# Rows of the split operands start behind 2 edge elements instead of 16, and both samples' rows get the edge

## The reference

```
ctx   = causal_ema(x, tau_ctx)
wg    = sigmoid([x, ctx] @ Wg.T + bg)
gated = x * wg
mod   = 0.5 + sigmoid(gelu(x @ Wn1.T + bn1) @ Wn2.T + bn2)     # 8 rates
temporal = sum over d of blend_d * causal_ema(gated * mod_d, tau_d)
gate  = sigmoid(temporal @ Wtemp.T + btemp)
soma  = gelu(x @ Wsoma.T + bsoma)
x     = x + layernorm((soma * gate) @ Wout.T)                  # stage 1

s0, s1, s2 = relu(x @ share_wi[i]) @ share_wo[i]               # F = 1024
expert_out = two experts of four, picked by the sample's type, weighted
g     = softmax(relu([first tokens] @ gate_w1) @ gate_w2)
x     = x + g0 * expert_out + g1 * s0 + g2 * s1 + g3 * s2      # stage 2
```

## Time and profile before

| | |
|---|---|
| median of 3 runs | 1089.53 us (1088.98 to 1089.96) |
| profiled execution | 1089.96 us |
| its span, first to last instruction | 1087.5 us |
| instructions | 12453, of them 4754 matmuls |
| granted TensorE clock | 1.00 on the mean |

### The profile page before, as it was taken

The page is one execution under the profiler, slowest core; times in us unless marked ns, Lnnn a source line. Parts: engine busy times, 40 slices in busy tenths (PEclk is TensorE's granted clock), DMA queues, the critical chain, the costliest instruction groups (busy, mean ns, idle before and its releaser), DMA issues.

```text
span 1087.5 us, 12453 instructions
## 1 busy us (share of the span) xinstructions
PE 1067.4 (98%) x4754; PEld 861.6 (79%) x4754; DVE 764.0 (70%) x1245; ACT 399.1 (37%) x628; POOL 8.9 (1%) x20
## 2 busy tenths in 40 slices
PE   8799999999999999999999999999999999999998
PEld 6388777888888888888888888888888888888886
DVE  7979987499654995469863896549955598545234
ACT  6454455422334233332344223432234323322231
POOL 0000000000000000000000000000000000000000
PEclk9999999999999999999999999999999999999999
DMA  6359888676444564546544564545645465446550
GB/s 219 112 198 388 304 322 303 240 292 254 143 170 160 206 254 155 175 154 255 190 155 155 198 249 172 189 160 194 234 152 194 155 237 209 144 168 220 184 193 19
DMA packets 36476, 219.58 MB, mean 202 GB/s; under 512 B 4354, under 2 KB 4610, under 8 KB 14786
## 3 DMA queue, kind: packets, MB, share of 16 engines
q1 hardware_dynamic: 34114, 206.22, 52.5%
q0 software_dynamic: 2304, 12.58, 3.1%
HBM read 185.10 MB, written 33.69 MB: 201 GB/s over the span
## 4 chain that ended last, share of the span: by engine, by line
PE 81%; DVE 16%; issue 1%; ACT 1%; DMA 0%; DVEq 0%
PE ps_up L583 12%; PE ps_up L585 12%; PE ps_up L584 11%; PE ps_down L584 11%; PE ps_down L585 11%; PE ps_down L583 11%; PE ps_aux L583 3%; PE ps_aux L585 3%; PE ps_aux L584 3%; DVE trace L1162 3%; DVE hid_lo L1065 3%; DVE trace L1193 2%; DVE temporal L1202 1%; DVE wi L1057 1%; PE ps_down L727 1%
## 5 line engine op out<-in xcount | busy, mean ns | idle before, releaser
L1065 DVE SCALAR_TENSOR_TENSOR hid_lo<-ps_up,hid_hi 128x512 fp32r<-128x512 f32 x320 | 219.5, 689 | 268.0 <-ACT hid_hi L863 266.2
L863 ACT ACTIVATE hid_hi<-ps_up 128x512 fp32r<-128x512 f32 x320 | 192.0, 600 | 544.9 <-PE ps_up L585 544.5
L583 PE MATMUL ps_up<-x_hi_all,wi 128*128 128x512 f32 (+1 forms) x644 | 256.6, 398 | 0.1
L585 PE MATMUL ps_up<-x_hi_all,wi 128*128 128x512 f32 (+1 forms) x644 | 253.5, 394 | 0.0
L583 PE MATMUL ps_down<-hid_hi,wo 128*128 128x512 f32 x640 | 250.6, 392 | 1.7 <-DVE hid_lo L1065 1.1
L584 PE MATMUL ps_down<-hid_lo,wo 128*128 128x512 f32 x640 | 250.9, 392 | 0.0
L585 PE MATMUL ps_down<-hid_hi,wo 128*128 128x512 f32 x640 | 250.5, 391 | 0.0
L584 PE MATMUL ps_up<-x_lo_all,wi 128*128 128x512 f32 (+1 forms) x644 | 249.8, 388 | 0.0
L583 PEld LDWEIGHTS ps_down<-hid_hi,wo 128*128 128x128 f32 x640 | 120.2, 188 | 31.0 <-issue 3.2
L585 PEld LDWEIGHTS ps_up<-x_hi_all,wi 128*128 128x128 f32 x644 | 120.7, 187 | 30.1
L584 PEld LDWEIGHTS ps_down<-hid_lo,wo 128*128 128x128 f32 x640 | 120.5, 188 | 27.8
(11 more groups left out here) (202 smaller groups left out, 836.8 us busy)
## 6 DMA issues: line engine op xcount, KB each, us to landing
wi<-split_wi SPq DMA_DIRECT2D x70, 1024.0 KB, 4.8
wo<-split_wo SPq DMA_DIRECT2D x70, 1024.0 KB, 4.9
modb<-mod_scratch SPq DMA_DIRECT2D x28, 512.0 KB, 4.4
split_wi<-wi SPq DMA_DIRECT2D x10, 1024.0 KB, 6.6
split_wo<-wo SPq DMA_DIRECT2D x10, 1024.0 KB, 8.2
xt<-in_x SPq DMA_DIRECT2D x8, 512.0 KB, 6.0
split_wi<-ex POOLq DMA_DIRECT2D x4, 1024.0 KB, 7.9
split_wo<-ex POOLq DMA_DIRECT2D x4, 1024.0 KB, 6.6
```

Of the source, the lines that this page charges most:

```text
L583: pe.matmul(ps, w_hi, x_hi, start=start, stop=False)
L585: return pe.matmul(ps, w_lo, x_hi, start=False, stop=stop)
L863: act.activation(hid_hi[:, k % NU, :], ps_up[k % NU][:, :], ACT.Relu).then_inc(hid_hi_ready, 1)
L1065: dve.scalar_tensor_tensor(hid_lo[:, k % NU, :], ps_up[k % NU][:, :], 0.0, f32(hid_hi[:, k % NU, :]), ALU.max, ALU.subtract).then_inc(hid_ ...
```

## The change

`EDGE` goes from 16 elements to 2. `x2_hi_all` and `x2_lo_all` become arrays of (parity, c, EDGE + T), so that each of their four rows has an edge, and the separate overlay for sample 1 goes: its split x is written and read as the rows of parity 1. The views `xg_hi`, `xg_lo`, `x2_hi`, `x2_lo` cover the same elements as before. On each partition the two buffers shrink from 2080 to 2056 elements, the `xg` ones from 1056 to 1028.

```diff
--- before.py
+++ after.py
@@ -98,7 +98,7 @@
 GATE_PART_SLOT = 31
 MIX_ORDER = (1, 2, 3, 0)
 HALF = T // 2
-EDGE = 16
+EDGE = 2
 FINAL_OWN = P
 
 AUX_BANKS = {"mod_hidden": (0,), "mod": (1,), "gate_hidden": (0,)}
@@ -174,8 +174,8 @@
 
         y = sb("y", [P, 5, CT, T])
         x2 = sb("x2", [P, 2, CT, T])
-        x2_hi_all = sb("x2_hi_all", [P, 2 * CT * T + CT * EDGE], F32R)
-        x2_lo_all = sb("x2_lo_all", [P, 2 * CT * T + CT * EDGE], F32R)
+        x2_hi_all = sb("x2_hi_all", [P, 2, CT, EDGE + T], F32R)
+        x2_lo_all = sb("x2_lo_all", [P, 2, CT, EDGE + T], F32R)
         xt = [sb(f"xt{i}", [P, CT, T]) for i in range(2)]
         xg_hi_all = sb("xg_hi_all", [P, CT, EDGE + T], F32R)
         xg_lo_all = sb("xg_lo_all", [P, CT, EDGE + T], F32R)
@@ -360,9 +360,7 @@
         final_gates = normed[:, :, :].rearrange("p t e -> p (t e)")
 
         xg_hi, xg_lo = xg_hi_all[:, :, EDGE:EDGE + T], xg_lo_all[:, :, EDGE:EDGE + T]
-        x2_hi, x2_lo = (t[:, 0:2 * CT * T].rearrange("p (n c t) -> p n c t", n=2, c=CT) for t in (x2_hi_all, x2_lo_all))
-        x1_hi_all, x1_lo_all = (t[:, CT * T:].rearrange("p (c t) -> p c t", c=CT) for t in (x2_hi_all, x2_lo_all))
-        x1_hi, x1_lo = x1_hi_all[:, :, EDGE:EDGE + T], x1_lo_all[:, :, EDGE:EDGE + T]
+        x2_hi, x2_lo = x2_hi_all[:, :, :, EDGE:EDGE + T], x2_lo_all[:, :, :, EDGE:EDGE + T]
 
         def x_of(n):
             return xt[n % 2][:, :, :]
@@ -678,7 +676,7 @@
                         pe.wait_ge(aux_free[1], p.aux[1]["mod"])
                     modulation(ps_aux[1][:, :]).then_inc(aux_ready[1], 1)
                 elif step == "wgate":
-                    xh, xl = (xg_hi_all, xg_lo_all) if n > 1 else (x1_hi_all, x1_lo_all)
+                    xh, xl = (xg_hi_all, xg_lo_all) if n > 1 else (x2_hi_all[:, 1, :, :], x2_lo_all[:, 1, :, :])
                     for m in range(CT):
                         if later(p.aux[m]["wgate"]):
                             pe.wait_ge(aux_free[m], p.aux[m]["wgate"])
@@ -733,7 +731,7 @@
                 pe.wait_ge(open_tsig, 2 + 2 * m)
                 stride = P if w == W_N1 else E
                 for c in range(CT):
-                    mm = context(bank[:, :], w + c * stride, x1_hi[:, c, :], x1_lo[:, c, :], c == 0, c == CT - 1, m)
+                    mm = context(bank[:, :], w + c * stride, x2_hi[:, 1, c, :], x2_lo[:, 1, c, :], c == 0, c == CT - 1, m)
                 return mm
 
             def opening():
@@ -998,7 +996,7 @@
                 wi_round(0)
 
                 act.wait_ge(x_loaded[1], 16)
-                hi(both(x1_hi), both(x_of(1))).then_inc(open_x1_hi, 1)
+                hi(both(x2_hi[:, 1, :, :]), both(x_of(1))).then_inc(open_x1_hi, 1)
                 wo_round(0)
                 wi_round(1)
                 for j in range(2):
@@ -1300,8 +1298,8 @@
                 step(dve.memset(eps[:, :], LN_EPS))
                 step(dve.memset(f32(xg_hi_all[:, :, 0:EDGE]), 0.0))
                 step(dve.memset(f32(xg_lo_all[:, :, 0:EDGE]), 0.0))
-                step(dve.memset(f32(x1_hi_all[:, :, 0:EDGE]), 0.0))
-                step(dve.memset(f32(x1_lo_all[:, :, 0:EDGE]), 0.0))
+                step(dve.memset(f32(x2_hi_all[:, 1, :, 0:EDGE]), 0.0))
+                step(dve.memset(f32(x2_lo_all[:, 1, :, 0:EDGE]), 0.0))
 
                 step(dve.tensor_reduce(soft[:, 0:2], par[:, C_BLEND:C_BLEND + CT * D].rearrange("p (c d) -> p c d", c=CT),
                                        AX_X, ALU.max, negate=True))
@@ -1466,7 +1464,7 @@
                     dve.wait_ge(open_temp_hi, c + 1)
                     lo(ct_lo[:, c, :], total[:, c, :], ct_hi[:, c, :]).then_inc(open_temp_split, 1)
                 dve.wait_ge(open_x1_hi, 1)
-                lo(x1_lo, x_of(1), x1_hi).then_inc(open_x1_split, 1)
+                lo(x2_lo[:, 1, :, :], x_of(1), x2_hi[:, 1, :, :]).then_inc(open_x1_split, 1)
                 for c in range(CT):
                     for h in range(2):
                         dve.wait_ge(open_tsig, 2 * c + h + 1)
```

## The result

| kernel | median | range of its runs |
|---|---|---|
| before | 1089.52 us | 1088.98 to 1089.96, 5 runs |
| after | 1095.53 us | 1094.18 to 1095.74, 5 runs |

The change makes the kernel slower: the ratio is 1.0052, 95% interval 1.0037 to 1.0067. The profiled execution of after took 1094.21 us, its span is 1092.3 us. Its lines are numbered two lower: L581 to L583 are the three matmuls of a product.

The account below looks back on a forecast made before the run. The prediction took TensorE's back-to-back matmul starts as the bound; its terms summed to 0 on the profiled 1089.96 us, and with the median 0.43 lower it forecast 1089.5 us, range 1083 to 1098.

Parts of the forecast that it names:

- What bounds the kernel: TensorE's matmuls stand back to back; 320 slots of 2.77 us make 886 us, the rest is opening and side work.
- Step 1: Moving reads of x2_hi and x2_lo in up: unaligned row starts cost 0, with bounds of -16 to +6.4 us.
- the last part: What would show the forecast wrong: starts settling at another pace for down too, which multiplies by 3840 and not 1920.
- slower by the up reads: Unaligned starts in up cost a stop or shift the weight-load rhythm: +6.4 us, 1096 us; chance 0.35 with weight loads.
- The faster one: Rival: up gains 3 ns a read, as wgate's shifted reads seemed to: -5.8 us, 1083.7 us; chance 0.23.
- The slow weight load in `out`: Rival: unaligned xg weight loads in out cost more, counting from 11 ns each; included in the slower case's 0.35.
- Step 2: xg operands: moving reads -0.8 to +0.5 us, weight loads in out up to 0.3 us; taken at 0.
- Steps 3 and 4: ScalarE and VectorE writes in two runs, and four smaller memsets saving at most 0.34 us: each taken at 0.
- Step 5: DMA: same transfers and sizes, destinations moved by multiples of 64 bytes; taken at 0.

Follow-up runs that it names:

- the ladder: Whole kernels against before, mostly with all x2_hi and x2_lo rows at one chosen place within 64 bytes, 2112 bytes apart; 1088.43 to 1102.06 us without moving hid.
- x2_at_32: Against before, all x2_hi and x2_lo rows start 32 bytes past a multiple of 64, 2112 bytes apart; 1094.66 us, ratio 1.0046.
- only_xg: Against before, only the xg rows get 2 elements of edge, x2_hi and x2_lo stay as before; 1090.58 us, ratio 1.0008.
- edge4: The changed kernel with EDGE = 4 instead of 2, so every x2 and xg row starts at a 16-byte unit; 1094.34 us, ratio 1.0042 to before.
- x2_at_20: Against before, all x2_hi and x2_lo rows start 20 bytes past a multiple of 64, 2112 bytes apart; 1102.06 us, ratio 1.0118.
- x2_hid_at_28: Against before, x2 rows start 28 bytes past a multiple of 64 and hid rows move to 12 bytes into a 16-byte unit; 1087.17 us, ratio 0.9979.
- x2_at_28: Against before, all x2_hi and x2_lo rows start 28 bytes past a multiple of 64, 2112 bytes apart; 1088.43 us, ratio 0.9989.

## Why the prediction was wrong

The forecast was no change, 1089.5 us; 1095.53 lies within the range of 1083 to 1098 and on the side that had a chance of 0.35.

**What bounds the kernel** was right: nothing but the distance of matmuls moved, and 320 slots times the change of one gives the loss.

**Step 1** failed, at this sentence: "I take the value of the steady slot, nothing added: the unaligned row lies inside the spread of the aligned ones". It priced starts at 8 to 56 bytes with a row at phase 60. That place, 12 bytes into a unit, belongs to the three cheapest of the ladder; no row of before showed another unaligned place, and the ladder spans 13.6 us. What the step set at 0 measured 320 x 17.4 ns = 5.6 us by the steady slots, and 5.1 us as the sum over all `up` and `down` matmuls of the two traces. The working had the right bound, 320 x 0.02 = +6.4 us, and took it for the rival only.

The step also counted stops of single reads. Near half of the loss is none: over the eight samples `up` grew by (3 x 13.3 + 5 x 5.8) / 8 = 8.6 ns a steady slot and `down` by 5 x 14 / 8 = 8.8 (over the whole trace 3.1 and 2.1 us), and `down` reads `hid` and `wo`, which did not move. That was named in the last part ("if the pattern of starts settles at another pace for `down` as well") and given no share of the forecast.

The Trainium skill's rule (SBUF — State Buffer, section Specifications (TRN2)) was weighed in step 1 as a count of lines. The runs agree so far as the place inside 16 bytes matters, and disagree with the count: a row 12 bytes in touches 129 lines like one 4 bytes in, and is 9.5 to 13.6 us faster in the ladder (1088.4 to 1089.8 against 1099.3 and 1102.1); rows that touch 128 lines take 1089.5 (before) to 1094.7 (`x2_at_32`). The estimate of 1091.2 us by it was 4.3 us short.

**The rival "slower by the up reads"** had the side and the size: +6.4 us was its price, +6.0 was measured. The size is partly luck: its price was the pace of twelve `soma` matmuls, at aligned rows. Its words "or shifts the rhythm" hold; its other half, a stop at an unaligned start, is not enough. The sign by which it was to be told (triples of c = 0 long, those of c = 1 not) came out the other way: in the even slot shown, c = 0 takes 0.69 us (397.95 to 398.64) and c = 1, whose rows start at a 16-byte unit, 0.72 (398.64 to 399.36). In the odd slots it does hold: there c = 0 grew by 6 ns and c = 1 not at all. A distance ends with the start of the next matmul and may hold that one's weights as well, so this alone convicts neither triple.

**The other rivals.** The faster one argued from the shifted reads of `wgate`, which were cheap; the place is cheap, but the change puts only the c = 1 shifted reads there and the c = 0 ones 4 bytes in. The slow weight load in `out` is refuted: 24 matmuls of `out` take 2.83 us in after (420.23 to 423.06), 2.85 before.

**Step 2**: bounds of -0.8 to +0.8 us together; `only_xg` gave +0.8 against its own runs of before (1089.76), interval -0.1 to +1.9, of which `wgate` explains 0.4. **Steps 3 and 4** were right to 2 ns: 1227 and 1225 ns for 1226, 1054 for 1056, four memsets together 0.09 us shorter. **Step 5**: no DMA wait appeared.

**What stays open.** Shown is that the loss is in the place of the `x2` rows, and that it lies in the pace of the whole stream of `up` and `down`. Not shown is which of the three things that moved (8 bytes into a unit for c = 0, other places within 64 bytes, a distance of 2056) carries how much: curing the first (`edge4`) gave back 1.2 us, less than the two intervals can tell apart; rows all 8 bytes in cost as much as after; and kernels with 16-byte starts alone, before among them, ranged from 1089.5 to 1094.7 us. No run moved the rows of one c alone, or the distance alone. Why the pace settles where it does was not found.

## What to carry to other kernels

Where matmuls stand back to back, a change of layout that adds no instruction can still change thousands of intervals: 3.6 ns on each of 3840 were 1.2% in `x2_at_20`. So measure start to start, and price a new row start by a row with the same place, not by another unaligned one; even that gives a pace to within some 27 ns a slot, as the two parities and sample 7 show. Don't assume that the cost sits on the matmul whose operand moved; look at its neighbours' pace too, as `x2_hid_at_28` shows. A sweep over the slots of one kernel finds candidates cheaply, but only whole kernels decide; here rows 12 bytes into a 16-byte unit for `x2` and `hid` are the best version found, 1087.17 us, 0.2% under before.

## What the runs showed of the hardware

- The steady slots of different layouts take few values: 2740, 2747, 2753, 2760, 2767, 2773, 2780, 2787, 2793, 2807 and 2813 ns among them. These are whole multiples of 6.67 ns, which is 16 periods of 2.4 GHz, the level of the granted clock in all these rows. The exceptions found are the slots that alternate: 2763 and 2790 in `edge4`, 2765 and 2802 in `x2_at_32`, and, by 1 to 3 ns, the even samples of `x2_at_28`.
- A matmul of 512 columns with its weight load stood 224 to 260 ns from the next in the slots read, 228 to 234 on the mean of a slot. The Trainium skill (TensorE: Matmul & The Clock Gate, section Back-to-back issue gap) gives 216 ns for an isolated gap and 131 for a stream; neither is what this trace shows.
- Moving `x2` by 8 bytes changed the time by 13.6 us, and one layout ran at two paces 27 ns a slot apart.
- Moving `hid`, which `down` reads, made `up` 2.0 us faster over the kernel and `down` none (`x2_hid_at_28` against `x2_at_28`).
